# A two-layer transformer block: the second layer's quantised cross-attention rewritten with features on the partitions

## The reference, cut to what matters

```
q, k, v = fq_sym(x @ Wq), fq_sym(ctx @ Wk), fq_sym(ctx @ Wv)   # one step each: largest absolute value / 127
w = softmax(q k^T * 16**-0.5)                                  # per head
w = fq_zero(w)                                                 # one step: largest weight of ALL heads and samples / 255
out = (w v) @ Wo + bo
```

## Time and profile before

| | us |
|---|---|
| median of 3 runs (lowest, highest) | 3719.68 (3715.29, 3727.21) |
| the profiled execution, its own time | 3716.17 |
| its span, first to last instruction | 3714.4 |
| busy: PE, weight loads, DVE, ACT, POOL | 2975.6, 1854.4, 2303.9, 1916.2, 724.2 |
| mean granted TensorE clock | 0.818 of 2.4 GHz |

### The profile page before, as it was taken

How to read it: one execution, slowest core, us unless ns; L and a number is a source line. 1 busy time by engine, 2 the same in 40 slices (tenths; PEclk the granted TensorE clock), 3 DMA queues, 4 the chain that set the end, 5 groups by cost and what they waited for, 6 DMA issues and landing times. The chain is left out here.

```text
span 3714.4 us, 51380 instructions
## 1 busy us (share of the span) xinstructions
PE 2975.6 (80%) x16324; PEld 1854.4 (50%) x16324; DVE 2303.9 (62%) x4118; ACT 1916.2 (52%) x3264; POOL 724.2 (19%) x1076
## 2 busy tenths in 40 slices
PE   5989999776969999979599996897750217699999
PEld 3744444464548888858111111223640104488888
DVE  4668888465533444346699996886653866344443
ACT  3438888532533323235599997996322325232322
POOL 1021111334440000000453511002330205300000
PEclk8979999887989999989555555666975559799999
DMA  6643333244730000015765436672324103201000
GB/s 182 208 143 105 104 108 105 63 117 127 184 88 18 9 17 8 0 57 153 175 156 115 114 63 88 79 98 48 89 75 152 28 11 73 45 17 32 16 23 15
DMA packets 477771, 307.04 MB, mean 83 GB/s; under 512 B 304150, under 2 KB 415982, under 8 KB 476942
## 3 DMA queue, kind: packets, MB, share of 16 engines
q1 hardware_dynamic: 471230, 288.64, 33.0%
q0 software_dynamic: 4240, 14.10, 1.3%
q10 hardware_dynamic: 2112, 1.97, 0.3%
HBM read 183.70 MB, written 118.78 MB: 81 GB/s over the span
## 5 line engine op out<-in xcount | busy, mean ns | idle before, releaser
L2053 DVE TENSOR_REDUCE neg_max<-nat 128x1 f32<-128x512 f32 x640 | 400.7, 682 | 65.0 <-PE nat L1919 64.9
L2248 PE MATMUL nat<-k_stack,q_stack 48*128 48x512 bf16 x640 | 380.7, 604 | 71.5 <-DMA k_stack<-k1w 30.8
L2282 DVE TENSOR_REDUCE m_all<-nat 128x1 f32<-128x512 f32 x640 | 423.3, 690 | 17.4 <-PE nat L2248 17.1
L2302 ACT ACTIVATE nat<-nat,m_all 128x512 f32<-128x512 f32 x640 | 427.7, 2129 | 2.3 <-DVE m_all L2282 2.3
L2302 ACT ACTIVATION_READ_ACCUMULATOR nat<-nat,m_all 128x1 f32 x640 | 403.7, 1674 | 0.0
L937 DVE SCALAR_TENSOR_TENSOR ff<-outp,bias,gel 128x512 f32<-128x512 f32 x160 | 120.1, 751 | 427.8 <-PE outp L407 427.8
L1992 ACT ACTIVATE probs<-sT 128x1024 f32<-128x1024 f32 x320 | 327.9, 1026 | 89.9 <-PE sT L1928 80.3
L2479 ACT ACTIVATE exps<-sT 128x1024 f32<-128x1024 f32 x320 | 296.3, 1083 | 15.6 <-PE sT L2419 13.7
L868 ACT ACTIVATE gel<-outp,bias 128x512 f32<-128x512 f32 x160 | 110.0, 687 | 360.6 <-PE outp L407 360.6
L749 POOL TENSOR_TENSOR rstd<-var_eps,neghalf 128x4 f32<-128x4 f32 x48 | 49.2, 1025 | 1147.6 <-DVE var_eps L919 1147.5
L872 ACT CAST ff_hi<-ff 128x512 fp32r<-128x512 f32 x160 | 99.2, 620 | 312.0 <-DVE ff L937 312.0
(11 more groups left out here) (444 smaller groups left out, 7000.5 us busy)
## 6 DMA issues: line engine op xcount, KB each, us to landing
v<-vpad SPq DMA_DIRECT2D x64, 320.0 KB, 2.8
q_stack<-q_part SPq DMA_DIRECT2D x90, 160.0 KB, 5.8
k_stack<-k1w SPq DMA_DIRECT2D x90, 160.0 KB, 10.6
q_stack<-q_hi SPq DMA_DIRECT2D x160, 64.0 KB, 2.5
k_stack<-k_hi SPq DMA_DIRECT2D x160, 64.0 KB, 2.2
v_stack<-v SPq DMA_DIRECT2D x40, 256.0 KB, 3.1
self_out<-o_nat SPq DMA_DIRECT2D x80, 128.0 KB, 2.0
attn_nat<-self_out SPq DMA_DIRECT2D x64, 160.0 KB, 2.9
```

The lines of the kernel that those rows point to most:

```text
L2053: dve.tensor_reduce(neg_max[:, n % 2, qt, 2 * pr + ab:2 * pr + ab + 1], nat[(16 * (n + 2) + t) % 3][:, :], AX.X, ALU.max, negate=True).the ...
L2248: pe.matmul(bank[i % NAT][:, :], q_stack[half, slot, g, pr, qt * P:(qt + 1) * P], k_stack[half, slot, g, pr, :], start=True, stop=True).th ...
L2282: dve.tensor_reduce(k.m_all[:, column(i // TILES, i % TILES)], bank[i % NAT][:, :], AX.X, ALU.max, negate=True).then_inc(s["e_max_ready"], 1)
L2302: act.activation(b[:, :], b[:, :], ACT.Exp, bias=k.m_all[:, col], accum_out=k.s_all[:, col]).then_inc(s["a_nat_free"], 1)
```

## The change

1. **Contexts at opening.** `first_loads` also loads layer 1's Wk2 and Wv2, and the opening `context_phase` computes both layers' keys and values from one turned context: 7 more products, copies by ACT, seven reductions by DVE, and four more stores (k21 as features x tokens, v21 as tokens x features).
2. **Self-attention out by features.** In the second pass of layer 1's self-attention the copy, the transposes and the scaling are replaced by one DVE scaling of the 128x512 bank; four DMAs store it as rows of 2 KB.
3. **Dense phases by feature.** Layer 1's dense "q" and "ff" load that layout in 3 DMAs a sample in place of 5, and ACT and DVE split it straight from SBUF; the 12 transposes a sample go. The next load waits for the split of all three tiles.
4. **Cross-attention anew.** `exact_cross_attention` replaces the seven blocks with two. A unit is one or two groups of 4 or 8 heads whose features lie together on 128 partitions; q is rounded once into `q_int` on chip, k is spread into `k_int` with a mask, so that one matmul of 128 rows gives eight (or four) heads at once. In pass 1 the negated maximum is added to the scores by matmuls of an identity with the maximum's high and low part. In pass 2 a second matmul of 128 rows, against a selection tile, adds the shift.
5. **Weights.** Only Wo2 and the first 256 rows of Wff2 are split during the cross-attention; the other 1024 rows are split by GpSimd in dense "ff", behind the bias additions and ahead of its loop.

```diff
-            first_loads(nc, s, k, [wk, wv, *ws], ctx_nat)
-            context_phase(nc, s, k, 0, wk, wv, k20, v20, ctx_nat, own)
+            first_loads(nc, s, k, [wk, wv, *ws, wk1, wv1], ctx_nat)
+            context_phase(nc, s, k, wk, wv, k20, v20, ctx_nat, own, wk1, wv1, k21, v21)
...
-            w2, wo2 = (Split(nc, s, own, x, w[x]) for x in ("Wff2", "Wo2"))
-            with ExitStack() as short:
-                wk, wv = (Split(nc, s, short, x, w[x]) for x in ("Wk2", "Wv2"))
-                load_weights(nc, s, [wk, wv])
-                context_phase(nc, s, k, 1, wk, wv, [k21], v21)
-            steps_phase(nc, s, k)
-            quantise_phase(nc, s, k, [(q21, q21w, 0), (k21, k21w, 1), (v21, v21w, 2)])
-            stats_phase(nc, s, k, True, [q21w], [k21w], next_weights=[wo2, w2])
-            weight_step_phase(nc, s, k)
-            attention_phase(nc, s, k, 1, True, [q21w], [k21w], v21w, cross_out)
+            wo2 = Split(nc, s, own, "Wo2", w["Wo2"], over=wq)
+            w2 = [Split(nc, s, own, "Wff2", rows(w["Wff2"], 0, 2 * P), over=wo)]
+            exact_cross_attention(nc, s, k, q21, k21, v21, cross_out_T, [wo2, *w2])
+            w2.append(Split(nc, s, own, "Wff2", rows(w["Wff2"], 2 * P, FF - 2 * P)))
...
+                if main == "ff" and loader:
+                    for i in range(len(loader.jobs) + 1):
+                        loader.turn(pool, i)
+                    loader.passed()
...
+                    def scale_output(n):
                         wait(dve, "a_pv_done", TT * (n + 1))
+                        if n >= 2:
+                            wait(dve, f"a_o_stored{n % 2}", 64 * (n // 2))
+                        dve.tensor_scalar(o_sb[:, n % 2, :], o_ps[n % 2][:, :], k.out_step, None, ALU.mult
+                                          ).then_inc(s["a_o_scaled"], 1)
```

Pass 1 of the new function (u is a unit, 40 in all; two matmuls of 512 columns fill `nat` or `low`):

```diff
+    PE  natural(u): wait "y_max" u-1;   scores(nat[u % 2], u, True)          # 2 bf16 matmuls
+    PE  lowered(u): wait "y_exp" u-1
+                    for name, part in (("y_hi", hi), ("y_lo", lo)):
+                        wait(pe, name, u + 1)
+                        for i in range(2):
+                            pe.matmul(low[u % 2][:, i, :], identr[:, :],
+                                      part[:, u % 2, VH * i:VH * i + VH].unsqueeze(2).broadcast_to([P, VH, CTX_TOK]),
+                                      start=(part is hi), stop=False)
+                    scores(low[u % 2], u, False)
+    PE  order: natural(0); then for every u: natural(u + 1), lowered(u)
+    DVE for every u: maximum(u), [place_k(u + 1) for u < 2], summed(u - 2), [round_q(next sample) every 5th]
+    ACT for every u: [lift(next sample) every 5th], exp of low[u % 2], 1024 columns
+    POOL for every u: hi(u), lo(u), halved(u - 1): 128x512 f32 add; loader.turn(u)
```

Pass 2:

```diff
+    PE  scores(u): for i in range(2): k_int x q_int (start), sel x shift_rows (stop), 512 columns each
+    PE  products(u - 3): 2 matmuls of 32 output rows, 512 columns; o_ps by feature
+    ACT exp of sT[u % 3], 1024 columns
+    DVE round (1024), and scale_output for each of 24 tiles (128x512), stored as rows of 2 KB
+    POOL rounds v in four parts, straight into v_int
```

More of the change, by code:

```diff
@@ L477, in _ @@
                     act.copy(hi[:, c, :], bank[c][:, :]).then_inc(s["c_hi"], 1)
[L478 to L481, removed]
+                for m, M in enumerate(FEAT_TILES):
+                    act.wait_ge(s["c_prod"], b["c_prod"] + m + 1)
+                    act.copy(k_hi[0:M, m, :], k_bank[m][0:M, :]).then_inc(s["c_khi"], 1)
+                for m, M in enumerate(FEAT_TILES):
+                    act.wait_ge(s["c_prod1"], b["c_prod1"] + m + 1)
+                    act.copy(k1[0:M, m, :], k1_bank[m][0:M, :]).then_inc(s["c_out1"], 1)
+                for t in range(TT):
+                    act.wait_ge(s["c_prod1"], b["c_prod1"] + 3 + t + 1)
+                    act.copy(v1[:, t, :], v1_bank[t][:, 0:D]).then_inc(s["c_out1"], 1)
             @block.vector
@@ L514, in context_phase @@
+                for t in range(TT):
+                    dve.wait_ge(s["c_out1"], b["c_out1"] + 3 + t + 1)
+                    dve.tensor_reduce(k.ctx_amax[:, 1, t:t + 1], v1[:, t, :], AX.X, ALU.max, apply_absolute_value=True)
+        for x, n in (("c_turned", 2), ("c_hi", 2), ("c_lo", 2), ("c_prod", 7), ("c_khi", 3), ("c_out", 7), ("c_vset", 2),
+                     ("c_prod1", 7), ("c_out1", 7), ("c_absmax", 1)):
             s.passed(x, n)
 def dense_phase(nc, s, k, layer, main, ln_g, ln_b, ws, wo=None, out_b=None, attn_in=None,
[L519 removed]
+                ff_bias=None, stores=None, final=None, next_weights=(), by_feature=False):
@@ L657, in _, with load_attn_T @@
             def _(sp):
+                def load_attn_T(b, split_b=None):
+                    if split_b is not None:
+                        sp.wait_ge(s["oT_split"], at["oT_split"] + split_b * 3 + 3)
+                    src = rows(attn_in, b * D, D)
+                    sp.dma_start(attn[:, 0:2, :], src[0:2 * P].rearrange("(c p) t -> p c t", p=P)
+                                 ).then_inc(s["attn_in_loaded"], 16)
+                    for half in range(2):
+                        sp.dma_start(attn[64 * half:64 * half + 64, 2, :], src[2 * P:D]).then_inc(s["attn_in_loaded"], 16)
                 def load_attn(b, turned_b=None):
+                    if by_feature:
+                        load_attn_T(b, turned_b)
+                        return
                     if turned_b is not None:
@@ L815, in step @@
                         pe.wait_ge(s["ff_split"], at["ff_split"] + b * FFC + m + 1)
+                        if loader and isinstance(b, int) and b == 0 and m == ws[1].full:
+                            pe.wait_ge(s["pool_split"], loader.split0 + len(loader.jobs))
                         for t in range(TT):
@@ L2118, in exact_self_attention @@
             **{f"a_v_loaded{r}": 16 * BATCH // 2 for r in range(2)},
-            **{f"a_o_stored{r}": 16 * NQ // 2 for r in range(2)}}
+            **{f"a_o_stored{r}": 64 * NQ // 2 for r in range(2)}}
         at = {name: s.before(name) for name in counts}
@@ L2458, in _ @@
                     wait(pe, "e_shift_turned", 3)
-                    for u in range(NU + UNITS + 1):
+                    for u in range(NU + LAG + 1):
                         if u < NU:
```

1221 lines of the change are left out of this document (460 added, 761 removed).

## The result

The changed kernel takes 3546.6 us (median of 4 runs, 3539.8 to 3548.5), the kernel before 3720.7 beside it: ratio 0.953, 95% interval 0.951 to 0.955. The forecast was 3502, its range 3455 to 3575. So the direction and the range hold, and 45 us of the forecast gain of 218 are missing. A second set of five runs of the changed kernel gave 3542.1 (ratio 0.952, 0.950 to 0.954).

What follows compares the result with a forecast made beforehand. Limits differ by stage; the 420.1 us cross-attention region, a row of hand-overs with no engine full, was to become 194. Terms +5 - 4 - 1 - 226 + 8 = -218 us gave 3498, forecast 3502, range 3455 to 3575.

Steps and rivals of the forecast that it cites:

- the closed loop through GpSimd's half sum: Cross-attention pass 1: exponential, GpSimd add, high and low parts, lowered matmuls bound the units; 2.3 us each, taken as 2.4.
- the loader: Cross-attention pass 1: GpSimd's jobs for Wo2 and 256 rows of Wff2, 14.6 us together, 9 counted on the path.
- all three are alike, so 1.2: Cross-attention pass 2: PE 1.1, ACT 1.1 and DVE 1.05 us a unit, so 1.2 a unit, 48 for 40.
- PE's own term: Cross-attention pass 2, a unit: four matmuls 0.9 us and two products 0.2, so 1.1 at full clock.
- what goes for certain is the last quad's tail: Self-attention's second pass: ACT's exponentials stay the bound, only 1.12 us of transposes, a copy and smaller stores go; -3 us.
- In this trace that costs nothing I can separate: Dense "q": the split reading SBUF for both inputs on DVE beside GpSimd was given no price; term -1 us.
- PE is not its limit: Dense "q": PE loses 12 transposes a sample, but is busy only 126 of 188 us; term -1 us.
- Dense "ff": GpSimd's loader jobs delay the first rstd, +16 us; fewer PE transposes save 7 x 1.3 = 9; taken as +8.
- (a): Rival: the new cross-attention passes stay at half clock, +40 us in pass 1, +44 in pass 2; 3586 us, chance 0.12.
- (b): Rival: cross-attention pass 1's loop costs more than its terms, 3.0 us a unit, +25; 3527 us, chance 0.15.
- (c): Rival: slower than before, as matmuls with the broadcast (zero-stride) operand are slow; 3758 us at 1.6 more each, chance 0.02.
- (d): Rival: the loops don't overlap, pass 1 takes its whole chain a unit, about 6.3 us, +156; 3658 us, chance 0.03.

Runs made afterwards that it cites:

- breaking it: Changed kernel with GpSimd's half sum one unit later in cross-attention pass 1 and three exponential buffers: 3543.4 us, stage 199.4 against 204.7.
- with the buffers: Changed kernel with four output buffers instead of two in self-attention's second pass: 3522.7 us, stage 323.0 against 329.2 in the kernel before.
- two pairs of kernels: Without against with idle transposes in dense "q": changed kernel, stage 196.3 against 188.8 us; kernel with four further edits, 197.2 against 188.4 us.
- the four edits that gained here: Changed kernel plus four output buffers, earlier scaling in pass 2, first rstd ahead in dense "ff", later half sum in pass 1; together 3485.5 us.

## Why the prediction was right, and where it was wrong

- **Cross-attention, pass 1 (forecast 124 us, 122.9 measured).** Right in its mechanism: the closed loop through GpSimd's half sum, added up as 2.3, taken as 2.4 and measured as 2.30, shown by breaking it. The first five units took 9.3 us more than that, against 9 forecast for the loader; GpSimd's split jobs and a clock of 0.58 lie there together. That the sum came out within 1.1 us is luck: the head was 20.3 us instead of 12 to the first exponential, as k's load landed only at 2805.2 behind q's; the tail was 3.7 instead of 7.
- **Pass 2 (69 with the gap, 81.8 measured).** The step "all three are alike, so 1.2" is the one that failed. It summed engines and did not follow the two `o_ps` banks: a bank's scaling stood one unit too late in DVE's order. Bubbles cost about 0.2 us a unit; without them it is 1.33, so 1.2 was also 0.1 short. That is PE's own term, taken as 1.1 and measured as 1.29: the forecast read four products inside 0.40 us as 0.2 for two. But those four start within 0.01 us of each other, and two take 0.39, so half the number is not half the time; in PE's order they cost 0.41.
- **Self-attention's second pass (-4, +15.8 measured).** The term "what goes for certain is the last quad's tail" was right about the removed work: with the buffers it is -6. What it missed is a wait that the edit tightened. The old wait for a store is in the code of before, and the diff moved the scaling ahead by three units and set four stores for one. None of the rivals named it; a look at what each wait of the new scaling is queued behind would have.
- **Dense "q" (-1, +8.3).** The sign was wrong, for two reasons. First, "In this trace that costs nothing I can separate": the forecast named the subtraction with both inputs in SBUF beside GpSimd and gave it no price. It takes 3.36 us instead of 0.69 there, and the first rstd came 3.8 us later, not earlier for two loads less. The trace of before had the sign of it: `ff_lo` (L940), with both inputs in SBUF, took up to 1.71 us beside GpSimd's bias addition, with a median of 0.69. Second, "PE is not its limit" was true of busy time and wrong of the stage: PE's part of each sample lies in the chain, and its clock depends on what else it does. In the earlier trace rows the clock was 0.84 at 67% busy; the change took the transposes that lay in the gaps, it became 0.81, and the seven distances grew by 4.6 us. That the clock carries this part is shown in the profiles of two pairs of kernels, its size in the median is not. The first part is read from traces with either form; no run moves the additions away from it here.
- **Dense "ff" (+8, +9.3).** Right in both parts: rstd(0) came 48.1 us after the stage's first issue instead of 29.0, so 19 for 16 (1.3 of the 3 are the bias additions, 24.2 us instead of 22.9, beside three slow subtractions), and a sample takes 60.21 instead of 61.55 us, 7 x 1.34 = 9.4 for 9.
- **Opening (+5, +5.6).** Right in what ends it, SyncE's four further stores, but they take 3.8 us instead of 2, and what stands ahead of the eight old ones costs 1.9 instead of 3; the two errors nearly cancel.
- **Rivals.** (a) is refuted by the clock, 0.91 and 1.00; (b) by 2.30 us a unit; (c) by 0.22 us a matmul; (d) by the spacing.

The total was within the range because the new cross-attention, by far the largest term, was worked out from its loops. The span came out 49 us above the forecast: 20 + 9 + 11 in the three failed steps, 2 in dense "ff" and the opening, 8 in unchanged code. The median is 45 above it, because the profiled execution stood 0.8 us above its median this time and 3.5 below it before.

## What to carry to other kernels

When an edit moves a step ahead in an engine's order, write down each wait it carries and what its releaser is queued behind. A store behind a batch of loads in one DMA queue is as late as the loads, and two buffers that were enough three units later are not enough now. An operand moved from PSUM to SBUF can change the price of an instruction beside GpSimd; look for what GpSimd does at that moment before it is put at nothing. Work laid out as a ring of two banks needs the whole cycle written down, not only the busiest engine: three of the four edits that gained here moved a step by one place or added a buffer. On GpSimd, put what the phase's start waits for ahead of what is only needed later.

## What the runs showed of the hardware

Taking work off PE can slow the work that is left: in dense "q" the granted clock fell from 0.84 to 0.81 and the samples' seven distances grew by 4.6 us; in self-attention's second pass it fell from 0.65 to 0.50, at no cost, as ACT was the bound. And transposes that compute nothing raised the clock in both places, 0.50 to 0.62 and 0.81 to 0.85. A DVE subtraction of 128x512 with both inputs in SBUF took 3.36 us beside GpSimd's additions of 128x1280, and 0.69 where GpSimd was idle or where one input came from PSUM. Two products of 32 output rows took 0.39 us where four started within 0.01 us of each other had taken 0.40. A matmul whose moving operand repeats each element 64 times costs the same 0.22 us as one that reads 512 different columns.
